# Second aggregation of a graph network: where the divisors of the softmax are added up and how they reach every partition

## The reference, cut to what matters

```
h = (x @ W1).reshape(1250, 4, 512)
e = leaky_relu(as_n[src] + ad_n[dst], 0.2)          # per edge and head
ex = exp(e - segment_max(e, dst)[dst])
denom = segment_sum(ex, dst)                        # one divisor per node and head
alpha = ex / (denom[dst] + 1e-16)
out = segment_sum(alpha[:, :, None] * h[src], dst)  # per node: heads * 512
h = elu(out + b1)
```

## Time and profile before

| | us |
|---|---|
| median of 3 runs (1906.89 to 1910.66) | 1908.12 |
| the profiled execution's own time | 1905.64 |
| its span, first to last instruction | 1903.9 |
| first to last product of this stage's line 1812 | 1270.0 to 1585.8 of the span |

### The profile page before, as it was taken

The page is one execution under the profiler, slowest core; times in us unless marked ns, Lnnn a source line. Parts: engine busy times, 40 slices in busy tenths (PEclk is TensorE's granted clock), DMA queues, the critical chain, the costliest instruction groups (busy, mean ns, idle before and its releaser), DMA issues. The chain is left out here.

```text
span 1903.9 us, 30552 instructions
## 1 busy us (share of the span) xinstructions
PE 1818.4 (96%) x11327; PEld 1757.4 (92%) x11327; DVE 1456.4 (76%) x2504; ACT 981.2 (52%) x1538; POOL 140.9 (7%) x139
## 2 busy tenths in 40 slices
PE   7999899998999999997999999989999998999998
PEld 5877699998999999996999889989999998999997
DVE  8888599998888988974555539658999995356766
ACT  4676421217898898865211232235677764232633
POOL 5110211201000000000011012100000000000000
PEclk9999999999999999998999999999999999999999
DMA  4221245454464435527554475562442407544302
GB/s 127 65 68 54 84 120 151 101 136 126 135 131 117 112 91 132 151 30 213 177 174 146 120 217 168 153 196 76 151 127 82 143 31 221 147 126 127 100 9 82
DMA packets 179273, 234.12 MB, mean 123 GB/s; under 512 B 75943, under 2 KB 151655, under 8 KB 178889
## 3 DMA queue, kind: packets, MB, share of 16 engines
q1 hardware_dynamic: 170407, 202.98, 38.9%
q0 software_dynamic: 7984, 27.24, 4.9%
q10 hardware_dynamic: 748, 2.10, 0.4%
HBM read 167.27 MB, written 65.00 MB: 122 GB/s over the span
## 5 line engine op out<-in xcount | busy, mean ns | idle before, releaser
L1812 PE MATMUL p_o<-p_hi,h_parts 125*128 125x416 f32 (+1 forms) x960 | 277.5, 356 | 6.9 <-DMA h_parts<-h_rows 5.2
L1138 PE MATMUL p_o<-first_room,p 125*125 125x193 f32 x1200 | 201.7, 329 | 5.7 <-ACT res L1020 2.9
L1138 PEld LDWEIGHTS p_o<-first_room,p 125*125 125x125 f32 x1200 | 196.9, 189 | 7.2 <-issue 6.7
L1138 PE MATMUL p_o<-h_in,p 125*125 125x193 f32 x1200 | 199.7, 329 | 2.9 <-ACT res L1020 2.9
L1138 PEld LDWEIGHTS p_o<-h_in,p 125*125 125x125 f32 x1200 | 197.6, 189 | 4.3 <-issue 3.1
L1812 PEld LDWEIGHTS p_o<-p_hi,h_parts 125*128 125x128 f32 x960 | 182.4, 190 | 13.6 <-DMA h_parts<-h_rows 5.7
L1088 DVE TENSOR_TENSOR e<-e 125x1250 f32<-125x1250 f32 x120 | 174.3, 1452 | 17.1 <-ACT e L1050 17.0
L885 PE MATMUL p_h<-pw_hi,x1T 128*125 128x384 f32 x720 | 186.9, 340 | 0.0
L781 DVE CUSTOM_DVE_ANT_0 max_junk<-src_row,G 125x1250 bf16<-125x1250 f32 x120 | 185.0, 1610 | 1.5 <-DMA src_row<-score_rows 0.9
L1474 PE MATMUL p_h<-pw_hi,x2T 128*125 128x256 f32 (+1 forms) x960 | 177.4, 286 | 4.4 <-DVE h_out L1430 4.4
L1093 DVE SCALAR_TENSOR_TENSOR p<-e,CT 125x1250 f32<-125x1250 f32 x120 | 175.3, 1461 | 4.6 <-PE p_o L1138 0.4
(11 more groups left out here) (293 smaller groups left out, 3762.0 us busy)
## 6 DMA issues: line engine op xcount, KB each, us to landing
f_raw<-turned SPq DMA_DIRECT2D x40, 500.0 KB, 9.3
h_parts<-h_rows SPq DMA_DIRECT2D x40, 448.0 KB
turned<-tail_room SPq DMA_DIRECT2D x18, 625.0 KB, 6.8
G<-turned SPq DMA_DIRECT2D x20, 562.5 KB
h_rows<-tail_room SPq DMA_DIRECT2D x22, 424.4 KB
h_rows<-h_out SPq DMA_DIRECT2D x16, 560.0 KB
h_rows<-tail_room SPq DMA_DIRECT2D x14, 560.0 KB
first_room<-in_w_gat POOLq DMA_DIRECT2D x36, 192.0 KB, 2.7
```

What stands on the lines that cost most here:

```text
L1138: last = nc.tensor.matmul(p_o[:, b, n * 256:n * 256 + C0 + 1], p[:, g % RING, d * T:(d + 1) * T], h_in[hh][:, s, 0:C0 + 1], start=(s == 0 ...
L1812: last = nc.tensor.matmul(p_o[:, bank(n, c), 0:w], h[:, s, kind, cols].bitcast(F32R), pp[:, g % RING, 0:w], start=(s == 0 and j == 0), sto ...
```

## The change

All ten tiles' weights are added on VectorE: `add` runs in steps 1 to 9, into one of two accumulators. The products with ones over the columns (`sum_weights`), the rounding of `acc` and `rest_of_sum` are gone. In a round's last step TensorE, ahead of the 12 products of the step, turns the finished `acc` to columns (`turn_sums`): four fp32 products, each with 105 columns of `acc` as the weights and two columns of ones passing, give sums of 105 destinations on 105 partitions. In step 3 of the next round VectorE adds 1e-16 and inverts these 105 by 4 numbers (`invert`). ScalarE multiplies an identity of 105 by 105 by each column of them (`diagonals`), and TensorE multiplies a matrix of ones by these four diagonals (`spread_sums`), so that the inverse of each destination stands on all 128 partitions. ScalarE copies it to SBUF (`keep_sums`), and `leave` waits for that copy. `spread_sums` of a round stands in TensorE's order behind the last step's 12 products and ahead of the next round's first. `diagonals` and `keep_sums` stand in ScalarE's step 3 behind `round_p`.

```diff
--- before.py
+++ after.py
...
@@ -1500,8 +1501,8 @@
     AHEAD = 2
-    ADDED = 4
-    SUM_AT = ADDED + 2
+    COLS = 105
+    PARTS = 4
     PER = CW + 1
...
@@ -1621,12 +1622,20 @@
 
+            def diagonals(n):
+                act.wait_ge(inverted, n + 1)
+                if n:
+                    act.wait_ge(spread_out, n)
+                for k in range(PARTS):
+                    last = a.activation(diagonal[:, k, :], core.ident[0:COLS, 0:COLS], ACT.Copy, scale=sum_cols[:, 1, k:k + 1])
+                last.then_inc(on_diagonal, 1)
+
             def keep_sums(n):
                 w = THIRDS[n % 3][1]
-                act.wait_ge(summed, n + 1)
+                act.wait_ge(spread_out, n + 1)
                 if n:
-                    act.wait_ge(inverted, n)
-                a.activation(sums[:, 0, 0:w], p_o[:, bank(n, CW), 0:w], ACT.Copy, bias=1e-16).then_inc(sum_kept, 1)
+                    act.wait_ge(left, n * CW)
+                a.activation(sums[:, 0:w], p_o[:, bank(n, CW), 0:w], ACT.Copy).then_inc(sums_left, 1)
 
...
@@ -1650,25 +1659,19 @@
                 a.activation(e[:, g % RING, 0:w], e[:, g % RING, 0:w], ACT.Exp, bias=col_src[1][:, i, s:s + 1]).then_inc(exp_ready, 1)
-                if g == 0:
-                    act.wait_ge(ones_set, 1)
-                    a.activation(ones[:], ones_f[:], ACT.Copy).then_inc(ones_set, 1)
                 if g:
                     round_p(g - 1)
                 if g == 3:
                     act.wait_ge(bias_in, 16)
                     a.activation(b_minus[:], b_col[:], ACT.Copy, scale=-1.0).then_inc(bias_in, 16)
                     act.wait_ge(bias_in, 32)
-                if s == ADDED:
-                    act.wait_ge(added, (n + 1) * (ADDED - 1))
-                    if n:
-                        act.wait_ge(p_used, (n - 1) * NT + SUM_AT + 1)
-                    a.activation(acc_hi[:, 0:w], acc[:, 0:w], ACT.Copy).then_inc(acc_hi_ready, 1)
                 if n and s == 3:
+                    diagonals(n - 1)
                     keep_sums(n - 1)
                 if n and 4 <= s < 8:
                     elu_exp(n - 1, s - 4)
             round_p(STEPS_ALL - 1)
+            diagonals(ENDS - 1)
             keep_sums(ENDS - 1)
...
@@ -1677,18 +1680,22 @@
             def invert(n):
-                w = THIRDS[n % 3][1]
+                dve.wait_ge(summed, n + 1)
+                v.tensor_scalar(sum_cols[:, 0, :], p_o[0:COLS, bank(n, CW), 0:2 * PARTS].rearrange("p (k a) -> p k a", a=2)[:, :, 0],
+                                1e-16, None, ALU.add).then_inc(sum_kept, 1)
                 dve.wait_ge(sum_kept, n + 1)
-                v.reciprocal(sums[:, 1, 0:w], sums[:, 0, 0:w]).then_inc(inverted, 1)
-                dve.wait_ge(inverted, n + 1)
+                if n:
+                    dve.wait_ge(on_diagonal, n)
+                v.reciprocal(sum_cols[:, 1, :], sum_cols[:, 0, :]).then_inc(inverted, 1)
 
             def leave(n, c):
                 w = THIRDS[n % 3][1]
+                dve.wait_ge(sums_left, n + 1)
                 if c < CW - 1:
                     dve.wait_ge(chunk_done, n * (CW - 1) + c + 1)
                 else:
                     dve.wait_ge(p_used, (n + 1) * NT)
-                v.tensor_tensor(place(n)[:, c, 0:w], p_o[:, bank(n, c), 0:w], sums[:, 1, 0:w], ALU.mult).then_inc(left, 1)
+                v.tensor_tensor(place(n)[:, c, 0:w], p_o[:, bank(n, c), 0:w], sums[:, 0:w], ALU.mult).then_inc(left, 1)
 
...
@@ -1718,23 +1725,17 @@
             def add(g):
-
                 n, s = divmod(g, NT)
                 w = THIRDS[n % 3][1]
                 if s == 1:
-                    if n:
-                        dve.wait_ge(acc_split, n)
+                    if n >= 2:
+                        dve.wait_ge(summed, n - 1)
                     before = e[:, (g - 1) % RING, 0:w]
                 else:
-                    dve.wait_ge(added, n * (ADDED - 1) + s - 1)
-                    before = acc[:, 0:w]
+                    dve.wait_ge(added, n * (NT - 1) + s - 1)
+                    before = acc[:, n % 2, 0:w]
                 dve.wait_ge(p_ready, g + 1)
-                v.tensor_tensor(acc[:, 0:w], before, e[:, g % RING, 0:w], ALU.add).then_inc(added, 1)
-
-            def rest_of_sum(n):
-                w = THIRDS[n % 3][1]
-                dve.wait_ge(acc_hi_ready, n + 1)
-                v.tensor_tensor(acc_lo[:, 0:w], acc[:, 0:w], acc_hi[:, 0:w].bitcast(F32), ALU.subtract).then_inc(acc_split, 1)
+                v.tensor_tensor(acc[:, n % 2, 0:w], before, e[:, g % RING, 0:w], ALU.add).then_inc(added, 1)
 
...
@@ -1748,10 +1749,8 @@
                     rest_of_p(g - 1)
-                if 0 < s < ADDED:
+                if s:
                     add(g)
-                if s == ADDED + 1:
-                    rest_of_sum(n)
                 if n and s == 3:
...
@@ -1778,22 +1777,29 @@
                     else:
-                        pe.wait_ge(sum_kept, m + 1)
-
-            def sum_weights(g, n, s, w):
-                if g == ADDED:
-                    pe.wait_ge(ones_set, 2)
-                if s == ADDED:
-                    bank_is_free(n, CW)
-                passing = [p_hi[:, g % RING, 0:w], p_lo[:, g % RING, 0:w]]
-                if s == SUM_AT:
-                    pe.wait_ge(acc_split, n + 1)
-                    passing += [acc_hi[:, 0:w], acc_lo[:, 0:w]]
-                for k, pp in enumerate(passing):
-                    last = nc.tensor.matmul(p_o[:, bank(n, CW), 0:w], ones[:], pp,
-                                            start=(s == ADDED and k == 0), stop=(s == NT - 1 and k == 1))
-                if s == NT - 1:
-                    last.then_inc(summed, 1)
+                        pe.wait_ge(sums_left, m + 1)
+
+            def turn_sums(n):
+
+                w = THIRDS[n % 3][1]
+                if n == 0:
+                    pe.wait_ge(ones_set, 1)
+                bank_is_free(n, CW)
+                pe.wait_ge(added, (n + 1) * (NT - 1))
+                for k in range(PARTS):
+                    at = min(k * COLS, w - COLS)
+                    last = nc.tensor.matmul(p_o[0:COLS, bank(n, CW), 2 * k:2 * k + 2], acc[:, n % 2, at:at + COLS], ones_f[:, 0:2],
+                                            start=(k == 0), stop=True, skip_group_check=True)
+                last.then_inc(summed, 1)
+
+            def spread_sums(n):
+                w = THIRDS[n % 3][1]
+                pe.wait_ge(on_diagonal, n + 1)
+                for k in range(PARTS):
+                    at, to = min(k * COLS, w - COLS), min((k + 1) * COLS, w)
+                    last = nc.tensor.matmul(p_o[:, bank(n, CW), k * COLS:to], ones_f[0:COLS, :], diagonal[:, k, k * COLS - at:to - at],
+                                            start=(k == 0), stop=True, skip_group_check=True)
+                last.then_inc(spread_out, 1)
 
...
@@ -1802,8 +1808,8 @@
                 pe.wait_ge(p_split, g + 1)
-                if s >= ADDED:
-                    sum_weights(g, n, s, w)
+                if s == NT - 1:
+                    turn_sums(n)
                 for c in range(CW):
...
@@ -1814,6 +1820,8 @@
                 last.then_inc(p_used, 1)
+                if s == NT - 1:
+                    spread_sums(n)
             pe.wait_ge(left, (ENDS - 1) * CW)
```

More of the change, by code:

```diff
@@ L1511, in aggregate_layer1 @@
         e = sb("e", [T, RING, W], F32)
-        acc = sb("acc", [T, W], F32)
-        acc_hi = sb("acc_hi", [T, W], F32R)
-        acc_lo = sb("acc_lo", [T, W], F32R)
+        acc = sb("acc", [T, 2, W], F32)
+        diagonal = sb("diagonal", [COLS, PARTS, COLS], F32)
+        sum_cols = sb("sum_cols", [COLS, 2, PARTS], F32)
         p_hi = sb("p_hi", [T, RING, W], F32R)
@@ L1517, in aggregate_layer1 @@
         ones_f = sb("ones_f", [T, 128], F32)
-        ones = sb("ones", [T, 128], F32R)
-        sums = sb("sums", [128, 2, W], F32)
+        sums = sb("sums", [128, W], F32)
         b_col, b_minus = core.b1_col, core.b1_minus
@@ L1531, in aggregate_layer1 @@
         added = sem("added")
-        acc_hi_ready = sem("acc_hi_ready")
-        acc_split = sem("acc_split")
+        on_diagonal = sem("on_diagonal")
+        spread_out = sem("spread_out")
+        sums_left = sem("sums_left")
         p_ready = sem("p_ready")
```

## The result

The changed kernel takes 1928.21 us in the median of 5 runs (1924.24 to 1930.13) against 1908.12; the ratio is 1.0101 with a 95% interval of 1.0081 to 1.0120. It is slower by 20 us, where 18.5 had been forecast. Ratios further down are against runs of the kernel before made beside each experiment (medians 1909.03, 1908.59 and 1906.80). One execution of all took 2584 us at a mean granted clock of 0.65, in the run with chunks 0 and 1 in the middle of step 4: its ratio leaves that one out, and its other five have the median 1892.87.

The account below looks back on a forecast made before the run. TensorE and VectorE were both taken as nearly full in a 25.90 us round. First end -1.6, ten rounds +18.2, last round -1.3 and clock +3.2 gave +18.5 on the 1908.12 median: 1926.6 us, range 1914 to 1936.

Parts of the forecast that it names:

- The chain of 3.25 us: VectorE stands still from small addition to first `z`, over diagonals, spread and copy: 3.25 us, between 2.7 and 3.8.
- TensorE's part: Within the chain: 0.18 us until TensorE's first spread record, then 0.92 for the eight records.
- The straight line from 193 over 128 to 105 columns: Spread records on TensorE: spacing of 0.163 us at 193 columns and 0.112 at 128 gives 0.094 at 105.
- Work plus trip: VectorE's round is its work, 24.5 us, plus the chain, 3.25: 27.7, or +18.2 over ten rounds.
- The waits of before are counted as gone: VectorE's earlier waits in a round, 1.1 us, vanish because additions lengthen its steps while ScalarE keeps its pace.
- TensorE's spare time: TensorE's work of 24.3 us a round fits into 27.7 with 3.4 to spare, so it reaches `spread_sums` early.
- The ends: First `z` of the stage comes 1.6 us earlier; the last round, decided by TensorE alone, is 1.3 shorter.
- The clock: Idle TensorE slows its clock, the spread in two or three rounds of ten and half the last stretch: +3.2 us.
- its upper bound: High end of the forecast range, 1936 us, with a trip of 3.6 us and a clock term of 7.
- C: Rival: TensorE decides, rounds go to 24.3 to 24.5 us, about -17; chance 0.05 for faster at all.
- B: Rival: every spread at slow clock, diagonals at upper bound, rounds 28.9 to 29 us: +25 to +36; chance 0.17.
- D: Rival: a shorter trip of about 1.7 to 2.2 us, time within 0.2% or a little over; chance 0.08.

Follow-up runs that it names:

- the run with chunks 0 and 1 in the middle of step 4: Changed kernel with the multiplication moved to step 4, but chunks 0 and 1 multiplied ahead of the rest of p, 2 and 3 at step's end: 1893.01 us, 0.9917.
- the clock held up: Changed kernel with 12 identity products ahead of the spread in rounds 0 to 10, keeping TensorE busy while it waits: 1926.14 us, 1.0094.

## Why the prediction was right

**The chain of 3.25 us** was the main term, and measured 3.40 where nothing disturbs it. Small operations 0.42 (0.42 forecast, hand-over included), diagonals 1.20 (1.15), ScalarE's copy with its hand-overs 0.58 (0.58). The hand-over of 0.05 in the first of these was not what its row shows (473.87 + 0.18 to 474.15 is 0.10), and it measured 0.03. TensorE's part came near (1.20 for 1.10) by two errors that cancel in part: its first record came 0.06 us behind the last diagonal, not 0.18, and the eight records took 1.14, not 0.92. The straight line from 193 over 128 to 105 columns didn't hold: records of 105 columns are 0.11 apart, like those of 128.

**Work plus trip.** VectorE's 24.5 + 3.4 = 27.9 is the undisturbed round of 27.85. The move of the multiplication showed that both terms are real: with the trip covered the work alone remains, 24.73 to 24.82. "The waits of before are counted as gone" held too: VectorE's wait for line 1652 isn't in the changed kernel, and comes back when additions are taken out.

**TensorE's spare time.** The turn takes 0.67 us (0.8 forecast), and TensorE idled 3.2 (3.4) at the ends that follow a round at full clock.

**The ends.** The first `z` came 30.6 us behind the stage's start, 2.0 less than before (-1.6 forecast). That such a difference of two executions comes so near is luck: this stretch took 29.7 and 34.2 us in two kernels with equal code up to there. The last round was 25.48 against 25.7, -0.2 where -1.3 had been worked out; the 1.1 that are missing are the slow clock, which the forecast carried in another term at half its value. With the clock held up this round is 24.38, as worked out.

**The clock.** That slow stretches eat up the idle time that makes them was argued from the earlier trace rows, and it is what the rounds show: they alternate. Its term was 3.2, and it measured 4.2: the spread was slow at five of ten ends, for its whole length at two. If each end had been slow, as the rule of the Trainium skill ("TensorE: Matmul & The Clock Gate", Part 1) was read there, it would have been 9. That part of the rule by which activity releases the throttled clock the trace bears out: 0.50 behind the idle time at 1414, and 1.00 again at 1442, with TensorE at work between them.

So the sum: -2.0 + 22.6 - 0.2 = +20.4 measured in the two profiled stages, +18.5 forecast. In ten rounds the undisturbed part is 19.5 for 18.2 (0.15 more in each trip), and the clock's 3.1 came on top; at the last end the clock hid the gain. The prediction's own terms for a round, 24.5 + 3.25 - 25.90, give 18.5 in ten rounds and not the 18.2 that it added up, and the terms named for its upper bound give 1934 and not 1936; neither changes the outcome.

**The rivals.** C failed as argued. Its condition, that VectorE has other work during the trip, is what the moved multiplication supplies, and then its sign comes out: 0.992. B didn't happen, D neither.

**What it didn't see.** The prediction told the loss as the trip's. But the kernel with the additions alone is as slow. On VectorE the change adds 3.0 of additions and 3.4 of trip, 6.4 in a round, and takes away 3.3 (the inversion, the rest of the sum); of the 3.1 left, 1.1 fill waits that were there, and 2.0 are the undisturbed 27.85 against 25.90. Neither part alone can be called the cause. Moving the multiplication removes the trip, and that by itself is enough to be faster than before. Whether the kernel before would gain from such a move too, no run shows.

## What to carry to other kernels

When two engines are both full, price a change on each of them, and add to an in-order engine's work the whole time for which it stands still for a trip over others, since neither hides the other. Then look whether the order can put work of its own into the trip: here the inversion one step earlier and the multiplications one step later turned 1.010 of the time before into 0.992, with the same operations. And ask of each engine on the trip what is queued behind its part: four activations of 1.1 us cost 0.9 us a round in one place of ScalarE's order and nothing in another.

## What the runs showed of the hardware

- Four fp32 products that pass 2 columns over 105 columns of weights cost TensorE 0.67 us (eight records, 0.09 apart from the second on). Four that pass 105 columns cost 0.81 us until the next product starts where they stand right behind others, and 0.91 behind idle time; the records there are 0.11 apart, no less than for 128 columns.
- An activation of 105 columns with a column as scale lasts 0.37 us, four in a row 1.20.
- In the changed kernel the granted clock fell to half at each of the 5 ends behind 3.0 to 3.2 us of idle TensorE, and at one of 5 behind 1.2 to 2.0 us; its rounds alternate by themselves. The length of the idle time alone doesn't decide: with the diagonals issued twice the clock stayed at 1.00 from 1478 to 1486 behind 3.08 us, and with five additions less it fell behind 1.89, 2.02, 2.03 and 2.05 us and stayed behind 2.06 and 2.08. What decides is open here. At half clock the spread of eight records took up to 2.03 us in place of 1.14.
- A `TENSOR_TENSOR` of 125 x 416 on VectorE rises from 587 to 1009 ns in the mean in a kernel in which GpSimd adds tiles of the same size.
